# A tile's transposes, context products and strip results, each one slot closer to its scores

## The reference

```
x = x + L0(gn(x))      # gn: mean and variance over groups of 4 channels and all pixels
x = x + L1(gn(x))
```

```
sim     = softmax(sum(unfold(key) * query, channels))   # over the 27 positions
context = sum(sim * unfold(value))
out     = conv1x1(context, w, b)
```

## Time and profile before

| | |
|---|---|
| median of 3 runs | 1666.94 us |
| the profiled execution | 1666.51 us, span 1664.8 us |
| mean granted TensorE clock | 0.998 of full |
| TensorE matmul busy | 1594.8 us (96%) |
| TensorE weight loads | 1331.8 us (80%) |
| VectorE busy | 1245.4 us (75%) |
| ScalarE busy | 1177.7 us (71%) |
| GpSimd busy | 792.6 us (48%) |
| DMA | 197.68 MB, 119 GB/s on average |

### The profile page before, as it was taken

How to read it: one execution, slowest core, us unless ns; L and a number is a source line. 1 busy time by engine, 2 the same in 40 slices (tenths; PEclk the granted TensorE clock), 3 DMA queues, 4 the chain that set the end, 5 groups by cost and what they waited for, 6 DMA issues and landing times.

```text
span 1664.8 us, 36807 instructions
## 1 busy us (share of the span) xinstructions
PE 1594.8 (96%) x10439; PEld 1331.8 (80%) x10439; DVE 1245.4 (75%) x4518; ACT 1177.7 (71%) x3044; POOL 792.6 (48%) x1759
## 2 busy tenths in 40 slices
PE   1799999999999999999999999999999999999998
PEld 1588888888888888888888888888888888888887
DVE  5477777777777777777777777777777777777675
ACT  2477677777677777677777777777777777777775
POOL 4554454454454455554454554454554454554430
PEclk9999999999999999999999999999999999999999
DMA  3134443444444444443444434344434344434233
GB/s 122 34 103 128 144 114 119 129 107 127 145 110 123 127 108 128 145 109 124 124 109 130 145 106 127 119 114 130 145 104 129 114 119 130 145 100 133 74 85 121
DMA packets 73558, 197.68 MB, mean 119 GB/s; under 512 B 11536, under 2 KB 52880, under 8 KB 65168
## 3 DMA queue, kind: packets, MB, share of 16 engines
q1 hardware_dynamic: 73360, 195.32, 40.1%
HBM read 51.62 MB, written 51.38 MB: 62 GB/s over the span
## 4 chain that ended last, share of the span: by engine, by line
PE 68%; POOL 18%; issue 7%; DVE 5%; ACT 2%; POOLq 0%; DVEq 0%; ACTq 0%
PE ps_s L384 16%; PE ps_o L417 15%; PE ps_v L451 10%; PE ps_p L434 9%; PE ps_t L396 7%; PE ps_p L429 6%; POOL hats L704 4%; POOL hats L703 2%; ACT hats L610 2%; DVE e L905 1%; POOL yb_row L744 1%; POOL xb_diag L745 1%; POOL hat_sum L706 1%; PE ps_v L477 1%; POOL g L685 1%
## 5 line engine op out<-in xcount | busy, mean ns | idle before, releaser
L549 ACT ACTIVATE e<-e,zmin 128x256 f32<-128x256 f32 x800 | 404.2, 505 | 258.5 <-DVE zmin L905 254.8
L417 PEld LDWEIGHTS ps_o<-eT,v 128*128 128x128 f32 x3584 | 478.1, 192 | 70.8 <-issue 69.8
L417 PE MATMUL ps_o<-eT,v 128*128 128x128 f32 (+1 forms) x3584 | 518.5, 272 | 0.4 <-ACT eT L564 0.4
L905 DVE CUSTOM_DVE_ANT_0 e<-ps_s,mask 128x256 f32<-128x256 f32 x800 | 334.6, 418 | 224.9 <-PE ps_s L384 216.9
L384 PE MATMUL ps_s<-kk,qq 128*128 128x256 f32 x1408 | 436.2, 392 | 2.1 <-DVE zmin L905 2.1
L918 DVE TENSOR_SCALAR e<-e,rz 128x256 f32<-128x256 f32 x800 | 361.2, 452 | 0.0
L564 ACT ACTIVATE eT<-ps_t 128x512 f32<-128x512 f32 (+1 forms) x416 | 235.9, 567 | 107.6 <-PE ps_t L396 103.4
L396 PE MATMUL ps_t<-ident,e 128*128 128x128 f32 x1600 | 305.7, 273 | 0.0
L396 PEld LDWEIGHTS ps_t<-ident,e 128*128 128x128 f32 x1600 | 225.2, 141 | 80.5 <-issue 0.2
L451 PE MATMUL ps_v<-wvox,xb 128*128 128x128 f32 x2048 | 272.4, 276 | 1.6 <-DVE v L937 1.4
L451 PEld LDWEIGHTS ps_v<-wvox,xb 128*128 128x128 f32 x2048 | 253.0, 193 | 15.8 <-issue 14.2
(11 more groups left out here) (154 smaller groups left out, 1636.9 us busy)
## 6 DMA issues: line engine op xcount, KB each, us to landing
raw<-in_x_dram SPq DMA_DIRECT2D x32, 1568.0 KB, 8.7
out_dram<-raw SPq DMA_DIRECT2D x32, 1568.0 KB, 5.4
v<-v SPq DMA_DIRECT2D x192, 256.0 KB, 3.7
kk<-kk SPq DMA_DIRECT2D x192, 112.0 KB, 2.2
ksp<-kk SPq DMA_DIRECT2D x192, 64.0 KB, 2.6
kk<-kk SPq DMA_DIRECT2D x32, 224.0 KB, 2.9
w_s<-in_w_dram SPq DMA_DIRECT2D x1, 64.0 KB, 6.4
wv_s<-in_wv_dram SPq DMA_DIRECT2D x1, 64.0 KB, 5.3
```

The source lines that it names most:

```text
L417: last = nc.tensor.matmul(o[:, UPIX * max(0, c - 1):UPIX * min(UNITS, c + 1)], v[:, s, c, :], eT[:, UPIX * (base + a):UPIX * (base + b)], ...
L549: nc.scalar.activation(e[:, i, :], e[:, i, :], ACT.Exp, bias=zmin[:, i:i + 1], scale=-1.0, accum_out=zs[:, i:i + 1]).then_inc(e_done.next( ...
L905: nc.vector.tensor_tensor_reduce(e[:, i, :], ps_s[(TILES * n.parity() + t) % 2][:, 0:KEYS], mask[:].rearrange("p s h a b -> p (s h a b)"), ...
```

## The change

Three constants are made smaller by one. Everything that goes by them is issued one slot earlier: the transposes and their copies two slots behind a tile's scores, the context products four, strip results and the store five. The scores, the masking, the exponentials, reciprocal and scaling, the projections, the values and the chain stay where they are. The run-out after the last image, FINAL + 1 slots, has one slot fewer.

```diff
-SCALE, TRANSPOSE, CONTEXT, FINAL = 1, 3, 5, 6
+SCALE, TRANSPOSE, CONTEXT, FINAL = 1, 2, 4, 5
```

## The result

The changed kernel takes 1690.61 us, the median of 4 runs (1689.19 to 1690.83), the kernel before 1667.29 beside it. The ratio is 1.0138, with a 95% interval of 1.0121 to 1.0156: slower, by 23 us where 34 were forecast.

What follows compares the result with a forecast made beforehand. TensorE bounds the kernel, waiting each image at L434 for hid. Copy 0.49 plus strip result 0.59 gave 1.08, with 0.07 for slot 15; 30 images made 34.5 us on 1666.5, so 1701.0 us, range 1683 to 1708.

Steps and rivals of the forecast that it cites:

- The bound: TensorE, busy 96% of the span, sets the time; it is late in every image at L434, 22.3 us in all.
- That hid and not GpSimd's L723 releases L434: L434 waits for hid, though its wait row names L723; VectorE's masking of tile 1 leads to hid.
- The copy ahead of hats, 0.49: In slot 21 a ScalarE copy precedes exponential and hats, delaying GpSimd's chain and VectorE's L974 by 0.49 us.
- rival A: Only one of the two delays, hats copy or strip result, reaches L434: 1684 or 1685 us; chance 0.18.
- Strip 5's result, 0.59: In slot 0 strip 5's result (L924) stands before tile 1's masking on VectorE, delaying it by 0.59 us.
- The two branches to L434: L434 follows hid (922.53) or the late transposes (922.40, with 0.15 added); hid stays last by 0.13.
- The rest of the image: Other slots absorb their delays, except slot 13, whose late exponential makes slot 15's transposes 0.07 us late.
- The number of images, and the run-out: The loss counts in 30 images, 32 passes less two before any transposes; the shorter run-out gains 0.
- The signs: Expected afterwards: period 51.1 to 51.2 us, later hats, L924 in slot 0, TensorE idle about 1.45 in slots 1, 2.
- B: Further small-margin transposes, as in slots 4 and 7, are late too: 0.3 us more per image, 1710; chance 0.10.
- C: TensorE catches up or the order does not bind, so the delay is absorbed: 1667 us; chance 0.06.
- D: Earlier copies and results make hid ready for L434, whose 0.37 us wait per image vanishes: 1655; chance 0.04.

Runs made afterwards that it cites:

- r2: Kernel before (lags 3, 5, 6) plus one unused 128x512 ScalarE copy ahead of slot 21's exponential and hats: 1679.83 us, ratio 1.0077.
- r3: Kernel before (lags 3, 5, 6) with strip 5's result alone issued one slot earlier, in slot 0, ahead of tile 1's masking: 1682.79 us, ratio 1.0093.
- r4: Kernel before (lags 3, 5, 6) with both the added copy ahead of hats and strip 5's result in slot 0: 1697.87 us, ratio 1.0187.
- r8: Kernel before (lags 3, 5, 6) with hats issued in slot 20, right behind the exponential: 1650.23 us, ratio 0.9898.
- r1: Changed kernel with strip results put back to lag 6 (lags 2, 4, 6): 1677.14 us, ratio 1.0059 to the kernel before.
- r5: Kernel before (lags 3, 5, 6) with ScalarE's copy and exponential exchanged in slot 6 alone: 1662.20 us, ratio 0.9970.
- r10: Kernel before (lags 3, 5, 6) with hats issued in slot 20 and VectorE's L988 ahead of its slot's masking: 1636.89 us, ratio 0.9824.

## Why the prediction was right or wrong

*The bound.* Right. TensorE sets the time, and it met the end of the hats chain in every image, at L434. r2, r3 and r4 show it without touching the lags, r8 by taking it away.

*That hid and not GpSimd's L723 releases L434.* Right: in the changed kernel L434 follows hid by 0.06 at 935.50, and the waits name hid.

*The copy ahead of hats, 0.49.* Right in place, 0.47 measured. The forecast carried it whole to L974; 0.37 arrived, since L706 lost the company of a scaling. The prediction named this kind of contention under rival A and gave a price only for the case that all of the shift is absorbed; 0.10 was, a fifth of the term.

*Strip 5's result, 0.59.* Right, 0.59 in the changed kernel and 0.59 alone in r3.

*The two branches to L434.* Right that hid is last and that the transposes' waits lie inside. The price of a late transpose, taken as 0.15 with its weights, fits: tile 24 was ready at 932.39, the transposes started at 932.44 and lasted 0.06 longer than others, 0.11 together. Once the result is taken away (r1), this branch sets 0.48 where rival A's sum had 0.63 with a hats term of 0.49; with 0.37 in it that sum gives 0.51.

*The rest of the image.* Half wrong. The 0.07 of slot 15 did not come: scores to scores of slots 9 to 21 take the same time. I had left the context products where they were; the one with six matmuls moved from slot 15 into slot 14 (1.24 to 1.47 us), so slot 15 starts 0.2 later against slot 14, and the scaling is in time. And I weighed the slots that got their copy and not those that lost it: the freed slot 6 moved a scaling out of GpSimd's way and gave 0.17 back (r5). I had noted that slot 8 gains margin and did not ask what else the earlier scaling changes.

*The number of images, and the run-out.* Right: 30 x 0.79 = 23.7 of 24.1.

*The sum.* 1.08 + 0.07 against 0.96 - 0.17: the mis-sized terms are 0.12 on the way to L974 (0.10 on GpSimd, by L706, and 0.02 in the copy), 0.17 by L735 and 0.07 by slot 15, together 0.36 of 1.15. All three were put too high, so no error hid another; the time is in the range because the range reached down to rival A.

*The signs.* Hats behind a copy, L924 between statistics and reciprocal, and the waits of L396 for L918 came as said. The period was to be 51.1 to 51.2 and is 50.82. TensorE's idle time in slots 1 and 2 was to grow from 0.37 to about 1.45 and is shown as 0.89. That is less than the delay of 0.96 at L434 would add to 0.37, because part of a wait is shown as a longer matmul.

*Rivals.* A's mechanism (contention that goes away) acted on a part of one term and not on the whole. B, C and D did not come. Against C stand the runs that only add a delay: 0.59 in r3 and 0.97 in r4 reached the period whole, and the stretches from L434 to slot 6 (6.91) and from L486 to slot 21 (24.78) stayed as long as before in the changed kernel and in r3, so TensorE caught nothing up. What its weight loads leave free (20% of the span) was no headroom here.

## What to carry to other kernels

When a queue's order is shifted, look less at the items that are now due earlier and more at whom each moved item now stands in front of: a single 0.67 us instruction, off every path itself, cost 16 us by its new place. Find the stretch where the bounding engine already waits, follow its chain back through all engines, and ask of every moved instruction whether it enters that chain; then ask of every place left empty what runs earlier there. And move the head of such a chain first: issuing three small ScalarE instructions behind the exponential of the slot before, where the engine waits anyway, and one VectorE instruction ahead of its masking, brought 30 us, more than the 23 that the shorter lags cost.

## What the runs showed of the hardware

- A GpSimd operation on one column takes 0.19 us alone and 0.34 where it begins 0.05 us behind VectorE's scaling of 128 x 256 (L735); a sum of 128 x 128 takes 0.455 and 0.59 (L706, 0.08 behind). Where GpSimd's L704 begins first, it is the scaling that takes 0.44 instead of 0.35. Moving the scaling of slot 7 away from L735 took 4.8 us off the kernel (r5).
- A wait's name moves with the order of the queue: one and the same delay was 33.9 us of waits before L434 in r4, and in the changed kernel 24.7 us before L396 and 1.4 before L434.
- TensorE ran a whole image of r10 with 49.20 us shown busy in 49.20 us at the full granted clock, with weight loads in 41.44 of them. Busy time as the profile shows it can hold a wait: slot 23 of r4 is 0.25 us longer than before (L435 starts 0.60 instead of 0.45 us after the context products ahead of it and lasts 1.02 instead of 0.92) and shows no idle time.
